# A gated recurrence whose small factors reach the partitions by DMA instead of by TensorE

## The reference, cut to what matters

```python
q, k, v = silu(conv4(x @ Wq.T)), silu(conv4(x @ Wk.T)) * scale, silu(conv4(x @ Wv.T))
a    = sigmoid(x @ Wa.T + ba)        # decay, one for each of 8 heads x 128 values
beta = sigmoid(x @ Wb.T + bb)        # rate, one for each head
def step(S, ins):
    err = einsum(k_t, S) - v_t
    S = a_t * S - b_t * k_t * err
    o_t = einsum(q_t, S)
o = (o - mean(o)) * rsqrt(var(o) + EPS) * ln_w + ln_b     # for each token and head
y = (o * sigmoid(x @ Wg.T)) @ Wo.T
```

## Time and profile before

| | us |
|---|---|
| median of three runs | 2226.3 (2220.9 to 2226.8) |
| profiled execution | 2221.0 |
| its span, first to last instruction | 2219.3 |
| first product of the recurrence's loop (L676) | 74.9 |
| last state update of the loop (L848) | 1186.5 |
| mean granted clock of TensorE over the span | 0.94 of full speed |

### The profile page before, as it was taken

The page is one execution under the profiler, slowest core; times in us unless marked ns, Lnnn a source line. Parts: engine busy times, 40 slices in busy tenths (PEclk is TensorE's granted clock), DMA queues, the critical chain, the costliest instruction groups (busy, mean ns, idle before and its releaser), DMA issues. The chain is left out here.

```text
span 2219.3 us, 44086 instructions
## 1 busy us (share of the span) xinstructions
PE 1982.7 (89%) x17014; PEld 1697.9 (77%) x17014; DVE 1408.6 (63%) x3137; ACT 1038.6 (47%) x2697; POOL 531.8 (24%) x889
## 2 busy tenths in 40 slices
PE   3799999999999999999996697999999999779996
PEld 3688888888888888888885565888888888757675
DVE  5677667776677776767764675666666666343334
ACT  2444555455554555545552234665665665221112
POOL 6244324444244443344422000000000000000000
PEclk9899999999999999999997798999999999989998
DMA  4111011110111101111010100000000000200000
GB/s 161 39 35 30 17 40 40 35 25 21 40 40 35 27 19 40 40 35 32 14 40 6 63 1 0 1 2 2 1 2 1 2 1 1 77 0 1 0 0 19
DMA packets 76163, 54.71 MB, mean 25 GB/s; under 512 B 6200, under 2 KB 72896, under 8 KB 74944
## 3 DMA queue, kind: packets, MB, share of 16 engines
q1 hardware_dynamic: 75968, 52.04, 8.9%
HBM read 50.45 MB, written 1.57 MB: 23 GB/s over the span
## 5 line engine op out<-in xcount | busy, mean ns | idle before, releaser
L577 POOL TENSOR_TENSOR kfull<-kt,pair_rows 128x512 f32<-128x512 f32 x128 | 146.8, 1147 | 629.7 <-ACT kt L368 621.0
L789 ACT COPY wt<-ps 32x128 f32<-32x128 f32 x512 | 130.4, 255 | 344.3 <-PE ps L694 341.0
L347 PE MATMUL ps<-xT,taps 128*128 128x128 f32 x2176 | 290.0, 278 | 0.0
L347 PEld LDWEIGHTS ps<-xT,taps 128*128 128x128 f32 x2176 | 276.1, 198 | 3.5 <-issue 1.0
L832 DVE TENSOR_TENSOR prod<-ps,mt 128x128 f32<-128x128 f32 x512 | 147.2, 287 | 140.8 <-PE ps L705 107.3
L1501 DVE TENSOR_REDUCE b_nmax<-ps 128x1 f32<-128x128 f32 (+7 forms) x256 | 180.6, 752 | 73.0 <-PE ps L1351 73.0
L1108 PEld LDWEIGHTS ps<-f_w,f_hT 128*128 128x128 f32 x1408 | 167.1, 193 | 31.9 <-issue 23.7
L1094 PE MATMUL ps<-xTn,f_w 128*128 x352 | 167.5, 612 | 25.2 <-PEq L1003 18.5
L1478 POOL COPY b_spread<-b_inv 128x256 f32<-128x256 f32 x64 | 25.8, 403 | 664.7 <-DVE b_inv L1504 664.7
L705 PEld LDWEIGHTS ps<-gq,wt 128*128 128x128 f32 x768 | 124.1, 201 | 68.3 <-ACT wt L789 68.3
L694 PE MATMUL ps<-ident,w 128*128 128x128 f32 x512 | 162.3, 317 | 8.1 <-DVE w L835 7.8
(11 more groups left out here) (212 smaller groups left out, 4120.5 us busy)
## 6 DMA issues: line engine op xcount, KB each, us to landing
decay<-ends_dram SPq DMA_DIRECT2D x256, 128.0 KB, 5.0
wtap<-in_taps SPq DMA_DIRECT2D x4, 1024.0 KB, 11.2
f_w<-in_f_w SPq DMA_DIRECT2D x2, 2048.0 KB
f_w<-in_f_w SPq DMA_DIRECT2D x2, 768.0 KB, 5.1
xT<-in_xT SPq DMA_DIRECT2D x2, 512.0 KB, 12.9
stream<-in_x_tok SPq DMA_DIRECT2D x1, 1024.0 KB, 11.8
wkv<-in_w_kv_up SPq DMA_DIRECT2D x1, 1024.0 KB, 8.1
out<-stream SPq DMA_DIRECT2D x4, 256.0 KB, 2.0
```

What stands on the lines that cost most here:

```text
L347: mm = pe.matmul(part, lhsT=taps[:, tap, t * P:(t + 1) * P], rhs=xT[:, :, columns(at_next) - LOOK + tap:columns(at_next) - LOOK + tap + TS ...
L577: nc.gpsimd.tensor_tensor(kfull[:, n % 4, :, :], kt[:, n % 2, :].unsqueeze(1).to_broadcast([P, G, P]), cst["pair_rows"][:, :].unsqueeze(2) ...
```

## The change

Rates, near sums and factors are made as a few rows and spread over the partitions by DMA through DRAM:

- item `b` is one product with 8 output rows, `n` four with 32 output rows each, `var` four products of 256 columns with 32 equal output rows each, by new weights `mean_rows` and a smaller `head_sum`. ScalarE takes each away once, into `rate_rows`, `near_rows` and `rstd`, which is now 128 x 256: four groups of 32 equal rows.
- SyncE stores them and loads them back broadcast: `sp_spread_rates` after the decay loads of chunk 1 of a strip, `sp_spread_rstd` after those of chunk 3. The loads are 256 KB twice (`rr`), 384 KB twice (`gn`) and 512 KB (`sq`) a strip.
- the ring items `rs0`, `rs1` and `yt` go; `wo` gives the output with tokens on partitions; the rest stands in another order.
- `pool_rstd` works on 128 x 256 and stands ahead of the copies in half 6.
- VectorE waits for the spreads: for the factors in half 0, for the rates and near sums where it waited for ring items before.

```diff
+        NEAR = B * NBLK * 6
+        PART = H * N // 4
+        rstd = sb("rstd", [P, PART])
+        rate_rows = sb("rate_rows", [H, N])
+        rates_dram = nc.dram_tensor("rates_dram", (2, H, N), F32).ap()
+        rstd_dram = nc.dram_tensor("rstd_dram", (2, P, PART), F32).ap()
+        near_rows = sb("near_rows", [P, NEAR])
+        near_dram = nc.dram_tensor("near_dram", (2, P, NEAR), F32).ap()
...
-        BY_DVE = ("rs0", "rs1", "yt") + PRODUCTS
-        BOTH = [["rs0", "rs1", "k0.0"], ["k0.1"], ["k1.0"], ["k1.1", "p0"],
-                [], [], ["a0"], ["a1", "p1"],
-                ["n0", "n1"], ["wo.0"], ["wo.1", "b0", "b1"], ["a2", "p2"],
-                ["c0", "yt"], ["n2", "n3"], ["b2", "b3"], ["a3", "p3"],
-                ["c1"], ["var.0"], ["var.1", "g0"], ["g1", "p4"],
-                ["q0.0"], ["q0.1"], ["q1.0", "q1.1"], ["p5", "v0.0"],
-                ["v0.1"], ["v1.0"], ["v1.1"], ["p6", "v2.0"],
-                ["v2.1"], ["v3.0"], ["v3.1"], ["dt", "p7"]]
-        POST = ("rs0", "rs1", "wo", "yt", "g0", "g1", "c0", "c1", "var")
+        BY_DVE = ("wo",) + PRODUCTS
+        BOTH = [["k0.0"], ["k0.1"], ["k1.0"], ["k1.1", "p0"],
+                ["q0.0"], ["q0.1"], ["b", "a0"], ["n", "a1", "p1"],
+                ["wo.0"], ["wo.1"], ["a2"], ["a3", "p2"],
+                ["g0.0"], ["g0.1"], ["c0"], ["p3"],
+                ["g1.0"], ["g1.1"], ["c1"], ["p4"],
+                ["var", "q1.0"], ["q1.1"], ["v0.0"], ["v0.1", "p5"],
+                ["v1.0"], ["v1.1"], ["v2.0"], ["v2.1", "p6"],
+                ["v3.0"], ["v3.1"], ["dt"], ["p7"]]
+        POST = ("wo", "g0", "g1", "c0", "c1", "var")
         both = Ring(BOTH, BY_DVE)
         only_pre = Ring([[x for x in part if x.split(".")[0] not in POST + PRODUCTS] for part in BOTH], BY_DVE)
-        only_post = Ring([["rs0", "rs1", "wo.0", "wo.1", "yt"], ["g0", "g1", "c0", "c1", "var.0", "var.1"]], BY_DVE)
+        only_post = Ring([["wo.0", "wo.1"], ["g0.0", "g0.1", "g1.0", "g1.1", "c0", "c1", "var"]], BY_DVE)
...
             if item == "var":
-                for h in {"0": range(H // 2), "1": range(H // 2, H)}[half]:
-                    if h == 0:
-                        vector, count = ring.kept(ring.done(f, "c1"))
-                        pe.wait_ge(S["ring_act"], count)
-                    mm = pe.matmul(out[:, h:h + 1], lhsT=sq[:, h * N:(h + 1) * N], rhs=cst["mean_col"][:, :], start=True,
-                                   stop=True, skip_group_check=True)
+                vector, count = ring.kept(ring.done(f, "c1"))
+                pe.wait_ge(S["ring_act"], count)
+                for u in range(4):
+                    mm = pe.matmul(out[32 * u:32 * u + 32, 0:PART], lhsT=cst["mean_rows"][:, :],
+                                   rhs=sq[:, u * PART:(u + 1) * PART], start=True, stop=True, skip_group_check=True)
...
-            elif kind == "r":
-                if f:
-                    pe.wait_ge(S["rstd_done"], f)
-                for u in range(4):
-                    h = 4 * int(j) + u
-                    mm = pe.transpose(out[:, u * P:(u + 1) * P], rstd[:, h:h + 1].to_broadcast([P, P]), cst["ident"][:, :])
             elif item == "wo":
                 pe.wait_ge(S["gated"], 2 * f + 2)
-                for h in {"": range(H), "0": range(H // 2), "1": range(H // 2, H)}[half]:
-                    mm = pe.matmul(out[:, 0:N], lhsT=wo[:, h, :], rhs=cs[:, h * N:(h + 1) * N], start=(h == 0), stop=(h == H - 1))
-            elif item == "yt":
-                vector, count = ring.kept(ring.done(f, "wo"))
-                pe.wait_ge(S["ring_act"], count)
-                mm = pe.transpose(out[:, 0:P], yT[:, :], cst["ident"][:, :])
...
-            elif kind == "n":
-                if j == "0":
-                    pe.wait_ge(S["near_done"], 3 * (f + 1))
-                for u in range(2):
-                    h = 2 * int(j) + u
-                    mm = pe.matmul(out[:, u * B * NBLK * 6:(u + 1) * B * NBLK * 6], lhsT=cst["head_sum"][:, h % 2, :],
-                                   rhs=near[:, h // 2, :, :, :].rearrange("p b n e -> p (b n e)"), start=True, stop=True,
+            elif item == "n":
+                pe.wait_ge(S["near_done"], 3 * (f + 1))
+                for g in range(G):
+                    mm = pe.matmul(out[32 * g:32 * g + 32, 0:NEAR], lhsT=cst["head_sum"][:, :],
+                                   rhs=near[:, g, :, :, :].rearrange("p b n e -> p (b n e)"), start=True, stop=True,
                                    skip_group_check=True)
+            elif item == "b":
+                mm = pe.matmul(out[0:H, 0:N].rearrange("p (b t) -> p b t", b=B), lhsT=wb[:, :],
+                               rhs=xT[:, :, columns(at_next):columns(at_next) + TS], start=True, stop=True, skip_group_check=True)
...
+                if f >= 1:
+                    act.wait_ge(S["rstd_stored"], 16 * f)
+                last_one = nc.scalar.copy(rstd[:, :], out[:, 0:PART])
+            elif item == "b":
+                if f >= 1:
+                    act.wait_ge(S["rates_stored"], 16 * f)
+                last_one = run(rate_rows[:, :], out[0:H, 0:N], ACT.Tanh, bias=bias_b[:, 1:2], scale=0.5)
+            elif item == "n":
+                if f >= 1:
+                    act.wait_ge(S["near_stored"], 16 * f)
+                last_one = nc.scalar.mul(near_rows[:, :], out[:, 0:NEAR], 0.5 / DK)
...
-                dve.wait_ge(S["ring_done"], ring.done(f, f"rs{q}"))
-                nc.vector.tensor_tensor(cs[:, part], cs[:, part], bank(ring, f, f"rs{q}"), ALU.mult).then_inc(S["ring_dve"], 1)
+                if f:
+                    dve.wait_ge(S["rstd_in"], 16 * f)
+                nc.vector.tensor_tensor(cs[:, part], cs[:, part], sq[:, part], ALU.mult).then_inc(S["scaled"], 1)
...
-                wait_kept(dve, ring, f, "b3" if half else "b1")
+                dve.wait_ge(S[f"rates_in{half}"], 16 * (f + 1))
...
-                wait_kept(dve, ring, f, "n3" if half else "n1")
+                dve.wait_ge(S[f"near_in{half}"], 16 * (f + 1))
...
-            ch.step(nc.gpsimd.tensor_scalar(rstd[:, :], var[:, :], EPS / DK, None, ALU.add))
-            nc.gpsimd.tensor_tensor(rstd[:, :], rstd[:, :], cst["minus_half"][:, :], ALU.pow).then_inc(S["rstd_done"], 1)
+            ch.step(nc.gpsimd.tensor_scalar(rstd[:, :], rstd[:, :], EPS / DK, None, ALU.add))
+            nc.gpsimd.tensor_tensor(rstd[:, :], rstd[:, :], cst["minus_half"][:, 0:1].to_broadcast([P, PART]),
+                                    ALU.pow).then_inc(S["rstd_done"], 1)
...
+        def sp_spread_rates(sp, ring, f, nx):
+            wait_kept(sp, ring, f, "b")
+            sp.dma_start(rates_dram[nx], rate_rows[:, :]).then_inc(S["rates_stored"], 16)
+            wait_kept(sp, ring, f, "n")
+            sp.dma_start(near_dram[nx], near_rows[:, :]).then_inc(S["near_stored"], 16)
+            sp.wait_ge(S["rates_stored"], 16 * (f + 1))
+            if f >= 1:
+                sp.wait_ge(S["m_done"], f)
+                sp.wait_ge(S["diag_made"], 2 * f)
+            for half in range(2):
+                heads = slice(half * H // 2, (half + 1) * H // 2)
+                sp.dma_start(rr[:, heads, :, :].rearrange("p h b t -> p (h b t)"),
+                             rates_dram[nx, heads, :].rearrange("h n -> (h n)").partition_broadcast(P)).then_inc(S[f"rates_in{half}"], 16)
+                if half == 0:
+                    sp.wait_ge(S["near_stored"], 16 * (f + 1))
+                rows = near_dram[nx].rearrange("(g r) e -> g r e", g=G)[half * G // 2:(half + 1) * G // 2, 0:2, :]
+                sp.dma_start(gn[:, heads, :, :, :].rearrange("p (g r) b n e -> p g (r b n e)", r=2),
+                             rows.rearrange("g r e -> g (r e)").partition_broadcast(P)).then_inc(S[f"near_in{half}"], 16)
+        def sp_spread_rstd(sp, f):
+            sp.wait_ge(S["rstd_done"], f + 1)
+            sp.dma_start(rstd_dram[f % 2], rstd[:, :]).then_inc(S["rstd_stored"], 16)
+            sp.wait_ge(S["rstd_stored"], 16 * (f + 1))
+            rows = rstd_dram[f % 2].rearrange("(j r) e -> j r e", j=4)[:, 0, :]
+            sp.dma_start(sq[:, :].rearrange("p (j e) -> p j e", j=4), rows.partition_broadcast(P)).then_inc(S["rstd_in"], 16)
...
+                    if c == 1:
+                        sp_spread_rates(sp, both, f, 1 - f % 2)
+                    if c == NC - 1:
+                        sp_spread_rstd(sp, f)
...
+                        pool_rstd(pool, ch, both, f)
                         pool_prepare(pool, both, f, nx, 0, (S["k_kept"], B * pc + pb))
                         pool_prepare(pool, both, f, nx, 1)
-                        pool_rstd(pool, ch, both, f)
```

More of the change, by code:

```diff
@@ L305, in pe_item @@
                 mm = pe.transpose(out[:, 2 * P:3 * P], keys[:, 0:P], cst["ident"][:, :])
-            elif kind == "r":
-                if f:
-                    pe.wait_ge(S["rstd_done"], f)
-                for u in range(4):
-                    h = 4 * int(j) + u
```

(38 more changed lines are left out.)

42 lines of the change are left out of this document (19 added, 23 removed).

## The result

The changed kernel takes 2760.3 us (2759.8 to 2762.0), against 2223.6 us of the kernel before in the same comparison: ratio 1.2416, 95% interval 1.239 to 1.2441, 24% slower.

What follows compares the result with a forecast made beforehand. Strips bound by two serial pieces, TensorE's rounds, then GpSimd's chain. 15 boundaries at 41.1 us (+616), last strip +38, after the loop +49, prologue +4: +707 on 2221.0 gives 2928, with 5.3 for the median 2933 us; range 2820 to 3060.

Steps and rivals of the forecast that it cites:

- What bounds the kernel: Each 69.2 us strip is two pieces in series: 46.1 us set by TensorE and its rounds, 23.1 us on GpSimd.
- The price of the power: GpSimd's power in half 6, from 8 to 256 columns: linear, 46.5 us, lengthening a strip by 45.2 us; chance 0.80.
- The upper end: All 1667 ns of GpSimd's 8-column power scale with columns: 208 ns a column, 53.3 us for 256.
- The rest of the chain: GpSimd's other work from scan to L527 keeps its times; the addition costs at most 0.4 us more; chain 68.3 us.
- The other piece: Slots 0 to 19, halves 0 to 4: TensorE loses 7.6 us of work and gains 3.5, net -4.1 us a strip.
- the far bound of -7.4: The other piece's saving a strip if two stretches at a low clock go as well.
- the two low stretches of the clock: TensorE's granted clock at 0.60 and 0.57 in a strip of the kernel before; two times 4 us cost about 3.3 us.
- The transfers: Stores and spreads of rr, gn and rstd: hidden or nearly within strips; 7.9 us for the factors' store and spread.
- The cheap power: Rival, chance 0.13: GpSimd's power takes 2.1 us, kernel 2181 us, or 2130 if the clock's low stretches go too.
- Grouped columns: Rival, chance 0.07: GpSimd's power works columns in groups of 16 or 32, taking 23 or 12 us; 2530 or 2335 us.
- the prediction's own break-even sum: Over 17 powers, 16 in the loop, the change breaks even at a power of 4.7 us, 18 ns a column.
- Late spreads: Rival, 0.02 within the cheap power's 0.13: VectorE waits for rr or gn in half 3, 7.9 us a strip, 2307 us.

Runs made afterwards that it cites:

- before_plus_power_128: The kernel before, plus one GpSimd power over 128 columns of a constant, ahead of its own factor work, into an unread tile: 2600.0 us in one run.
- copies_before_power: The changed kernel with the factor's addition and power of 256 columns behind the sixteen copies again: 2815.0 us, 1.2675 of the kernel before.
- small_power_q0_late: small_power with ring item q0 moved back from slots 4 and 5 to 20 and 21: 2107.5 us, 0.9492 of the kernel before.
- small_power_more_products: small_power with item b making its product 8 times and item n its four products twice: 2127.1 us, 0.9578 of the kernel before.
- small_power: The changed kernel with the variances sent through DRAM into a 128x8 tile, so addition and power take 8 columns: 2103.1 us, 0.9464 of the kernel before.

## Why the prediction was wrong, point by point

**What bounds the kernel: right.** The GpSimd chain between scan and L527 set the strips. before_plus_power_128 shows it on the old kernel, and TensorE's stop at p7 is where it was put.

**The price of the power: the mechanism right, the size off.** This is the step that failed. The step "the 1447 ns scale, 181 ns a column, 0.22 + 256 x 0.181 = 46.5 us" took the fixed part from ordinary operations, 220 ns. Measured at 8, 64, 128 and 256 columns it takes 1.67, 10.89, 20.73 and 41.48 us, a line of 160.5 ns a column over 383 ns through the two outer points, with the inner two 0.2 us above and below it. The fixed part of this operation is larger than that of its neighbours; on 8 columns this is 163 ns, times 256 / 8 it is 5.2 us. Seventeen times 5.0 us are 85 us, the largest single share of the 173 between forecast and time. The upper end, 208 ns a column, stretched the range upwards by 116 us, the wrong side. Downwards it kept only "a little below for a fixed part between the two readings", and there the power alone took 85. Of the 10.1 us by which a strip was forecast too long (41.1 against 31.0), 5.0 are the power, 2.3 the rest of the chain and 2.8 the piece before it.

**The rest of the chain: a term missing.** "The chain becomes 23.06 - 1.67 + 46.5 + 0.4" kept its other parts unchanged. They took 18.5 us in place of 21.2: copies 3.99 (5.25), value products 2.37 (3.16), `kfull` 1.04 (1.20 and 1.38). While TensorE stands, so do VectorE and ScalarE, and GpSimd is faster alone: copies_before_power puts the copies back beside the working engines, and they take 5.33. That is 2.7 us a strip. The addition took 1.02 us, not 0.64.

Single records say which neighbour it is. In the loop of the kernel before, copies take up to 760 ns where VectorE works on two inputs that both lie in SBUF (`gn`, `rr`, `mt`, `tmp`, L482 to L504). They take at most 316 ns beside its other operations, which read `ps` or reduce, and at most 319 ns alone. VectorE pays too: its step on `tmp` takes 1.51 us beside the value products (L501 above). Beside the power it doesn't:

```profile
738.00 0.63 DVE L499 SCALAR_TENSOR_TENSOR tmp<-tmp 128x256 f32<-128x256 f32 x1
```

**The other piece: -4.1 forecast, -6.9 measured** (46.1 to 100.2 - 61.0 = 39.2 us), near the far bound of -7.4. Two of its terms can be read. The four products of item `n`, and the four of `var` behind the loop (eight records each):

```profile
791.42 0.39 PE L333 MATMUL ps<-xT,wb 128*8 128x128 f32 x2
...
793.79 0.53 PE L329 MATMUL ps<-near,head_sum 128*32 128x192 f32 x8
...
1698.36 0.64 PE L301 MATMUL ps<-sq,mean_rows 128*32 128x256 f32 x8 [1.39 <-ACT sq L390]
```

Eight `near` records read 0.53 us, and the next instruction starts 0.46 us after the first of them, against 1.45 us in the earlier trace rows; `n` was priced at 1.45: -1.0 us. The price held for products with 128 output rows; these write 32 rows each, into four different groups. The Trainium skill, "TensorEngine Tiling (Array Packing)", section "Overview", gives up to four times for outputs of at most 32 columns of the array, and the trace agrees with about three (1.45 / 0.46). And the two low stretches of the clock of the earlier trace rows are gone, worth up to 3.3 us by the prediction's own price, while the restart costs about 2.2 (2.10 us of work at 0.50 and 4.00 at 0.71, an estimate from the stretches above). Together that is -6.2 of the -6.9. The price of the low stretches is argued: small_power_q0_late has one of them back at well under 1 us a strip. Why they went is shown in part, by the place of q0 for the one in half 1; for the other it stays open. That TensorE's work sets this piece holds for about four fifths, by small_power_more_products.

**The transfers: hidden as forecast, a little longer than priced.** Median us to landing, beside the earlier trace rows:

```profile
gn<-near_dram SPq DMA_DIRECT2D x34, 384.0 KB, 6.4
sq<-rstd_dram SPq DMA_DIRECT2D x17, 512.0 KB, 7.5
```

Within the changed kernel's strips the only wait for a spread is one of 0.4 us. But 512 KB took 7.5 us against 6.1 taken. Behind the loop they are in the open, timeline of the last factors:

```profile
1699.06 0.37 ACT L369 COPY rstd<-ps 128x256 f32<-128x256 f32 x1 [0.84 <-PE ps L301]
...
1700.46 41.15 POOL L565 TENSOR_TENSOR rstd<-rstd,minus_half 128x256 f32<-128x256 f32 x1
...
1750.91 1.29 DVE L423 TENSOR_TENSOR cs<-cs,sq 128x512 f32<-128x512 f32 x2 [57.41 <-DMA sq<-rstd_dram]
```

From `var` kept (1699.43) to the first multiplication 51.5 us; the power is 41.15 of it. From the power's end, store and spread take 9.3 us, 7.9 forecast.

**The rivals.** The cheap power fell by the first row. Its case, worked out as 2181 us, or 2130 without the low clock, is what small_power makes real: 2103 us, with the clock at 1.00 in 15 of 16 strips. Grouped columns fell by the four points within 0.23 us of a line; their times were a little off (by the prediction's own break-even sum about 2540 and 2345 us, not 2530 and 2335), which changes nothing. The Trainium skill's 2.6 cycles an element ("GPSIMD Engine Reference", section 3.1) does not hold for this operation, which takes 160.5 ns a column where an ordinary one takes 1.59. That section of the Trainium skill gives the figure for an ordinary two-input add, and not, as the prediction put it, whatever is computed. Section 2.1 of the same page of the Trainium skill, an ordinary loop over elements, agrees with the line. Late spreads are seen only where the order was turned back.

## What to carry to other kernels

An operation priced on a small tile has to be asked what part of its time is fixed; two widths of the same operation settle it. Where the trace has only one, the range must reach down as well as up: here 163 ns more of fixed part, times 32, were 5.2 us an operation. Count the columns on one partition, not the numbers: 1024 numbers as 128x8 take 1.7 us here, as four rows of 256, each on 32 partitions, they take 41.5. And when one engine is stopped for long, don't carry the durations of the engine that runs on from the busy trace: it may run faster alone, and TensorE comes back at half clock (0.50 here). Last, look at every strip before you call a clock stretch gone or back: two neighbouring strips of one run differed here.

## What the runs showed of the hardware

- GpSimd's power of two operands costs 160.5 ns a column of 128 partitions, about a hundred times the 1.59 ns of an ordinary two-input operation, in a line from 8 to 256 columns (1.67, 10.89, 20.73 and 41.48 us).
- Sixteen copies of 64x128 on GpSimd take 3.99 us with VectorE silent and 5.25 to 5.33 us beside it; the two 128x480 products 2.36 against 3.16 us. Single copies are slow (up to 760 ns) only beside operations of VectorE with two inputs in SBUF, and stay at 316 ns or less beside those that read `ps` or reduce.
- VectorE's step of two inputs in SBUF takes 1.51 us beside GpSimd's 128x480 product and 0.63 us beside GpSimd's 41 us power.
- Four products of 192 columns that write 32 output rows each, in four groups of rows, take 0.46 us by the distance of starts; four that write 128 rows take 1.45 us.
- Two strips of small_power_q0_late have TensorE 2.46 of 4 us busy at the same place; the next 4 us had a granted clock of 0.57 in the one and of 1.00 in the other.
